# Attention of a two-layer kernel: the last five heads by halves of queries, nine scores in two slots, another end of the projection

## The reference, cut to what matters

```python
def _L0_attn_a_ref(x, Wk, Wq, Wv, Wu, bu):      # HEADS = 16, s = 8, t = 2048, e = 128
    scale = 1.0 / math.sqrt(s)
    keys = x @ jnp.triu(Wk).T                    # then reshaped to (b, t, h, s)
    queries = x @ jnp.tril(Wq).T
    values = x @ Wv.T
    dot = jnp.einsum('bqhs,bkhs->bhqk', queries, keys) * scale
    att = jax.nn.softmax(dot, axis=-1)
    out = jnp.einsum('bhqk,bkhs->bqhs', att, values).reshape(b, t, e)
    return out @ Wu.T + bu
x = x + _L0_attn_a_ref(_layernorm(x, axis=-1), ...)
x = x + _L0_ffn_ref(_layernorm(x, axis=-1), ...)
```

## Time and profile before

| | us |
|---|---|
| median of three runs | 1668.0 |
| the profiled execution's own time | 1668.66 |
| its span | 1666.9 |
| TensorE busy | 1519.7 (91%) |
| VectorE busy | 1383.8 (83%) |
| ScalarE busy | 920.8 (55%) |
| the tail, from the last maximum of the first pass (663.3) to the last instruction of the block (715.9) | 52.6 |

### The profile page before, as it was taken

How to read it: one execution, slowest core, us unless ns; L and a number is a source line. 1 busy time by engine, 2 the same in 40 slices (tenths; PEclk the granted TensorE clock), 3 DMA queues, 4 the chain that set the end, 5 groups by cost and what they waited for, 6 DMA issues and landing times. The chain is left out here.

```text
span 1666.9 us, 24179 instructions
## 1 busy us (share of the span) xinstructions
PE 1519.7 (91%) x8562; PEld 759.0 (46%) x8562; DVE 1383.8 (83%) x2459; ACT 920.8 (55%) x1751; POOL 296.9 (18%) x364
## 2 busy tenths in 40 slices
PE   6899999999999999979997888976999869989699
PEld 2111111111111111268883333322888758869587
DVE  6999999999999999476664999999766657787686
ACT  3088888888888888832224765754322232222232
POOL 3200000000000000000013788784000200020000
PEclk7599999999999999989998999999999979999799
DMA  3340000100000001000001222220000003200123
GB/s 95 102 159 24 24 30 27 31 27 25 24 24 24 24 24 49 9 1 1 1 1 41 73 64 72 67 67 26 1 1 1 1 1 103 81 23 1 52 78 103
DMA packets 41315, 65.92 MB, mean 40 GB/s; under 512 B 11444, under 2 KB 18661, under 8 KB 40490
## 3 DMA queue, kind: packets, MB, share of 16 engines
q1 hardware_dynamic: 41194, 64.37, 12.6%
HBM read 56.68 MB, written 6.75 MB: 38 GB/s over the span
## 5 line engine op out<-in xcount | busy, mean ns | idle before, releaser
L844 DVE TENSOR_REDUCE row_max<-ps 128x1 f32<-128x1024 f32 x512 | 601.2, 1220 | 33.4 <-PE ps L641 17.4
L758 ACT ACTIVATE probs<-ps 128x512 f32<-128x512 f32 x944 | 487.8, 603 | 119.7 <-PE ps L656 119.4
L641 PE MATMUL ps<-k_stack,q_stack 48*128 48x512 bf16 x1024 | 325.0, 402 | 20.4 <-DVE row_max L844 10.6
L656 PE MATMUL ps<-q_stack,k_stack 51*128 51x512 bf16 x944 | 322.1, 387 | 2.2 <-ACT probs L758 0.2
L585 PE MATMUL ps<-probs,v_head 128*16 128x512 f32 x2048 | 269.8, 599 | 1.3 <-issue 1.1
L641 PEld LDWEIGHTS ps<-k_stack,q_stack 48*128 48x128 bf16 x1024 | 58.5, 95 | 368.0 <-DVE row_max L844 342.0
L1373 PE MATMUL ps<-s_hc,ident 128*128 128x512 f32 x256 | 139.0, 628 | 47.9 <-DVE s_hc L1646 42.9
L1026 ACT ACTIVATE x_gate<-ps 128x512 f32<-128x512 f32 x128 | 76.5, 599 | 184.5 <-PE ps L122 184.4
L1298 POOL TENSOR_TENSOR s_dbx<-s_dx,s_b_rows 128x512 f32<-128x512 f32 x128 | 159.4, 1270 | 35.2 <-DVE s_h L1637 34.7
L1637 DVE TENSOR_TENSOR_SCAN s_h<-ps,s_state,s_dbx 128x512 f32<-128x512 f32 x128 | 157.3, 1274 | 4.6 <-POOL s_dbx L1298 2.8
L1063 DVE TENSOR_TENSOR x_hidden<-x_gate,ps 128x512 f32<-128x512 f32 x128 | 87.2, 686 | 53.4 <-PE ps L122 42.5
(11 more groups left out here) (345 smaller groups left out, 1935.1 us busy)
## 6 DMA issues: line engine op xcount, KB each, us to landing
s_b_rows<-s_b_dram SPq DMA_DIRECT2D x64, 256.0 KB, 3.1
y_spread<-y_probs_dram SPq DMA_DIRECT2D x128, 128.0 KB, 2.9
q_stack<-q_parts_dram SPq DMA_DIRECT2D x30, 96.0 KB
k_stack<-k_parts_dram SPq DMA_DIRECT2D x30, 96.0 KB
w_w<-w_dram SPq DMA_DIRECT2D x1, 2048.0 KB, 8.0
q_stack<-q_parts_dram SPq DMA_DIRECT2D x30, 64.0 KB
k_stack<-k_parts_dram SPq DMA_DIRECT2D x30, 64.0 KB
o_dram<-o_sb SPq DMA_DIRECT2D x60, 32.0 KB
```

Of the source, the lines that this page charges most:

```text
L641: last = nc.tensor.matmul(core.ps[:, 2 * b + r, :], qst[buf][0:KROWS, u * P:(u + 1) * P], kst[buf][0:KROWS, key:key + CH], start=True, sto ...
L656: nc.tensor.matmul(core.ps[:, S_BANK + n % S_RING, :], kst[buf][HALF:ROWS, kt * P:(kt + 1) * P], qst[buf][HALF:ROWS, c * CH:(c + 1) * CH], ...
L758: nc.scalar.activation(probs[:, us % RING, c * CH:(c + 1) * CH], core.ps[:, S_BANK + n % S_RING, :], ACT.Exp).then_inc(exp_done, 1)
L844: nc.vector.tensor_reduce(mx[:, u, b:b + 1], core.ps[:, 2 * b:2 * b + 2, :], mybir.AxisListType.XY, ALU.max).then_inc(max_done, 1)
```

## The change

The heads 11 to 15 go by halves of the queries: in the second pass, first all 16 key tiles for chunks 0 and 1, then all 16 for chunks 2 and 3, and the maxima of the 8 query tiles of a half are joined, turned, cut, stored and loaded by themselves. A score is then called an entry (1024 in all), and a list worked out ahead says how many are issued by the end of each slot: four more in every slot from 20, and a fifth in every even slot from 186 (HASTE), as far as the maxima are known by slot number (for a half of head h from slot 16h + 12 and 16h + 20). That makes 978 by slot 255, so that 46 are left for the tail. The fifth score stands behind the four pairs, ahead of the values.

The values of the halved heads go by groups of two entries: four matmuls of 256 columns for each (in place of four of 512 for a unit), eight entries behind the scores. So most slots have two groups; 14 even ones from 200 on have three, slot 196 has a whole unit and a group, slot 192 two whole units.

In the end, SyncE loads the 14 sums of weights alone as 112 rows of 256, VectorE takes one reciprocal of 112x256, SyncE stores it and loads it back spread over the eight rows of each head. The first half of head 15 is copied out (128x256) before its second half, and projected and added behind four of the tail's scores; `project_out` has two banks in turn and stands behind the scores with 9 and 5 left, behind the last score, and ahead of the last group of values. Only the second half of head 15 is left after the last exponent: one copy of 128x256, 8 small matmuls, four times a reciprocal and two tiles to add. The statistics and the tiles of the next norm's first chunk come ahead of that. The tail has five banks in place of six. The rolled numbering (bodies of 48 slots) is written out by entries; for heads 0 to 10 it gives the same order as before up to slot 185.

```diff
-    TAIL = UNITS - LAG_S
-    TAIL_BANKS, EARLY_OUT_BANK, LAST_TILES = (6, 4, 5, 0, 1, 2), 3, 3
-    OUT_UNITS = range(UNITS - NC_ - 1, UNITS - 1)
+    HALVED, HASTE = 11, 186
+    PAIR, QUARTER = 2, CH // 2
+    entries = [(head, kt, c) for head in range(HEADS)
+               for cs in (((0, 1), (2, 3)) if head >= HALVED else ((0, 1, 2, 3),))
+               for kt in range(NT) for c in cs]
+    def known_from(n):
+        head, half = n // OF_HEAD, n % OF_HEAD // OF_HALF
+        return head * NT + (LAG_S if head < HALVED else (half + 1) * (NT // 2) + LAG_S - NT)
+    issued = []
+    for gs in range(UNITS):
+        n = issued[-1] if issued else 0
+        if gs >= LAG_S:
+            most = n + NC_ + (gs >= HASTE and gs % 2 == 0)
+            while n < most and known_from(n) <= gs:
+                n += 1
+        issued.append(n)
+    TAIL = issued[-1]
+    TAIL_BANKS = tuple(S_BANK + (TAIL + i) % S_RING for i in range(S_RING)) + (0, 1)
+    LAST_HALF_BANK = 2
+    OUT_BANKS, END_BANKS = (3, 7), (0, 1, 4, 5)
...
             sp.wait_ge(o_stored, O_STORE * (HEADS - 2))
-            for which, dst in enumerate((attT, den)):
-                sp.dma_start(dst[0:MOST, :], od[which, 0:HEADS - 2]).then_inc(fin_loaded, 16)
-            store_max(HEADS - 1, (HEADS - 1) % NBUF)
-            store_o(HEADS - 2)
+            sp.dma_start(rden_rows[0:MOST, :],
+                         od[0:HEADS - 2, HD].rearrange("h (k n) -> h k n", n=QUARTER)).then_inc(den_loaded, 16)
+            sp.dma_start(attT[0:MOST, :], od[0:HEADS - 2, 0:HD]).then_inc(fin_loaded, 16)
+            store_max(LAST, 0)
+            store_max(LAST, 1)
+            sp.wait_ge(rden_ready, 1)
+            sp.dma_start(rdd.rearrange("h (k n) -> (h k) n", n=QUARTER), rden_rows[0:MOST, :]).then_inc(rden_stored, 16)
+            store_o(LAST - 1)
+            sp.wait_ge(rden_stored, 16)
+            sp.dma_start(den[0:MOST, :], rdd.unsqueeze(1).to_broadcast([HEADS - 2, HD, T])).then_inc(rden_loaded, 16)
...
+            def weigh_values(entry):
+                nonlocal weighed
+                while weighed < ENTRIES and weighed + group_size(weighed) <= entry:
+                    head, kt, c = entries[weighed]
+                    buf, half = head % NBUF, c // PAIR
+                    split = head >= HALVED
+                    bank = LAST_HALF_BANK if head == LAST and half else O_BANK
+                    if kt == 0 and c == 0:
+                        pe.wait_ge(v_staged, head + 1)
+                        if head:
+                            pe.wait_ge(evacuated, head)
...
+                    size = group_size(weighed)
+                    pe.wait_ge(exp_done, weighed + size)
+                    ring, at = weighed // NC_ % RING, weighed % NC_ * CH
+                    wide = size * CH // NC_
+                    out = half * wide if split and bank == O_BANK else 0
+                    for g in range(NC_):
+                        last = nc.tensor.matmul(core.ps[32 * g:32 * g + VROWS, bank, out:out + wide], v_head[buf][:, kt, :],
+                                                probs[:, ring, at + g * wide:at + (g + 1) * wide],
+                                                start=kt == 0, stop=kt == NT - 1)
+                    last.then_inc(pv_done, 1)
+                    weighed += size
...
+                first, end = issued[gs - 1] if gs else 0, issued[gs]
                 for c in range(NC_):
+                    find(c // 2, c % 2)
+                    if first + c < end:
+                        score(first + c)
+                for n in range(first + NC_, end):
+                    score(n)
+                weigh_values(end - 2 * NC_)
...
+            for n in range(TAIL, ENTRIES):
+                tail_score(n)
+                if n % 2:
+                    weigh_values(n + 1 - 2 * NC_)
+                left = ENTRIES - n
+                if left in (18, 17):
+                    project_first_half(18 - left)
+                if left in (14, 13):
+                    project_first_half(16 - left)
+                if left == 9:
+                    project_out(0)
+                if left == 5:
+                    project_out(1)
+            project_out(2)
+            weigh_values(ENTRIES - PAIR)
+            project_out(3)
+            weigh_values(ENTRIES)
+            pe.wait_ge(evacuated, HEADS + 1)
+            for g in range(NC_):
+                project_half(1, g, END_BANKS[g])
...
+            for n in range(ENTRIES):
+                head, kt, c = entries[n]
+                if n % OF_HEAD == 2 * NC_ and head:
+                    act.wait_ge(pv_done, group_of(head * OF_HEAD))
+                    if head > 1:
+                        act.wait_ge(o_stored, (head - 1) * O_STORE)
+                    nc.scalar.copy(o_sb[:], core.ps[:, O_BANK, :]).then_inc(evacuated, 1)
...
-            for c in range(NC_):
-                cols = slice(c * CH, (c + 1) * CH)
-                if c == 0:
-                    dve.wait_ge(fin_loaded, 32)
-                nc.vector.reciprocal(den[0:MOST, cols], den[0:MOST, cols]).then_inc(rden_ready, 1)
-                dve.wait_ge(rden_ready, c + 1)
+            dve.wait_ge(den_loaded, 16)
+            nc.vector.reciprocal(rden_rows[0:MOST, :], rden_rows[0:MOST, :]).then_inc(rden_ready, 1)
+            dve.wait_ge(fin_loaded, 16)
+            dve.wait_ge(rden_loaded, 16)
...
+            for g in range(NC_):
+                add_half(0, g, OUT_BANKS[g % len(OUT_BANKS)])
+            dve.wait_ge(half_added, 2 * NC_)
+            add_out(0)
+            dve.wait_ge(out_added, 1)
+            following.stat_rows(dve, 0)
+            add_out(1)
+            add_out(2)
             following.norm_rows(dve, 0)
+            add_out(3)
+            dve.wait_ge(out_added, NC_)
+            for g in range(NC_):
+                add_half(1, g, END_BANKS[g])
```

385 lines of the change are left out of this document (188 added, 197 removed).

## The result

**Slower, by about as much as forecast.** The median of the kernel after is 1679.34 us (1677.65 to 1682.16, 4 runs), that of the kernel before, measured beside it, 1667.39 (1666.19 to 1668.85, 4 runs): +12.0 us, ratio 1.0073, 95% interval 1.0055 to 1.0091. The prediction had +13.2, and 1681.

The account below looks back on a forecast made before the run. The prediction took a TensorE-ScalarE loop through three banks to bound each slot, with VectorE following. Main slots +28.9 and tail -15.7 gave +13.2 us on the median 1668.0, so 1681 us; own range 1673 to 1690, widened to 1666 to 1692.

Parts of the forecast that it names:

- The loop: Main slots: first score, its exponent, fourth score, values bind TensorE and ScalarE at 2.44 us a slot; VectorE follows.
- The fifth score: Even slots 186 to 254: waits for the second score's exponent, starts 0.48 later than the fourth did; +16.8 us.
- Values out of the tail: Main slots: 34 entries, 17 groups of 2 at 0.44 us each, move in from the tail; +7.5 us.
- Halved passes: Main slots: two more value passes per four entries, 0.013 us each, in some 60 slots; +1.6 us.
- rounds of maxima: Main slots: five more rounds of maxima at 0.1 us each; +0.5 us, ends 0 and 2.5.
- The copies: Main slots, heads 11 to 15: ScalarE's copies of bank 7 delay values or exponents; +2.8 us, ends 0 and 4.
- The tail: Last maximum to block end: 36.9 us against 52.6, with TensorE standing from T + 15 to T + 18.7; -15.7 us.
- the clock: Behind the block: gap shrinks to about 3 us, up to 3 us could be won, but 0 taken.
- VectorE's pace: Rival, main slots: VectorE paces them, so extra scores are hidden and the total is 1655 us; chance 0.14.
- a balance: Rival: even-slot waits partly taken up, tail gains 18 and clock 3; total within 0.2%, chance 0.06, slightly below 0.02.
- SyncE's order: Rival: SyncE's order holds maxima back until a slot stands; 1690 us and more, chance 0.03.
- Issue: Rival: issuing 16 value matmuls bounds halved slots, +0.5 us in 60 slots, 1711 us; chance 0.05.

Follow-up runs that it names:

- Experiment 2: Kernel before, each maximum taken over 512 of its 1024 columns, matmuls kept; 1657.90 us, one run.
- experiment 5: Kernel before, each slot's values weighed in two parts, half the columns behind the second find and score, half at the slot's end; 1629.66 us, ratio 0.9774.
- experiment 1: Kernel after without any fifth score (HASTE past the last slot), 80 entries left for the tail; 1667.73 us, ratio 1.0008.
- experiment 11: Kernel after, sums of heads 0 to 13 loaded spread out with `attT` and used undivided, no load back from DRAM; 1674.90 us, ratio 1.0044.
- experiment 6: Experiment 1's kernel with `project_out` sooner, tail values two groups at a time, head 14's output stored behind the spread load; 1663.20 us, ratio 0.9976.
- experiment 8: Kernel after, head 14's output stored between the last head's maxima so the spread load goes sooner; 1680.18 us, ratio 1.0079.

## Why the prediction was right, point by point

**What bounds a slot.** Right. The loop was read from the earlier trace rows against the waits, which named VectorE. Experiment 2 takes VectorE's load nearly in half and the slot stays; experiment 5 takes half of the values out of the loop and the slot falls to 2.27. The loop had forecast both; a VectorE that paced would have shortened every slot in the former and none in the latter.

**The fifth score.** The mechanism is shown (0.06 behind the second exponent). The size was 0.48 for each pair of slots, and measured is 2.93 + 2.40 - 2 x 2.444 = 0.44: the long slot is the 2.92 of the forecast, and the short one behind it gives back 0.04, since there VectorE waits and all four `find`s run without a stop. "The following slot of four gives nothing back" was the wrong sentence. Over the 35 pairs (two early ones have 0.37) it comes to some 15.2, where 16.8 was said. Slot 251 is 0.4 shorter, where 0.3 was said.

**Values out of the tail.** 0.44 a group was said, 0.43 measured: 7.3 for 7.5. **Halved passes** were +1.6 and **rounds of maxima** +0.5: experiment 1 has 0.5 for both in the five heads, and 0.9 with the second head. Two groups of values take 0.99, two passes took 0.98 (477.37 to 478.35). **The copies** and whatever else remains: 25.3 - 15.2 - 7.3 - 0.9 + 0.4 (slot 251) = 2.3, where +2.8 was said. The slots around the five copies are longer than their neighbours of the same kind by 0.9, 0.7, 0.1, 1.2 and 0.7, in all 3.7, but the 0.35 that each head of experiment 1 takes beyond its 16 slots (39.45 against 39.10) is gone from them. So the 3.6 too much in the first pass is 1.6 in the fifth scores, 1.2 in the passes and rounds, and the rest in small parts.

**The tail.** -15.7 was said, -11.4 came. Three steps of it: TensorE was to run into the wait at T + 15 and did so at T + 16.2 (1.2 of the 4.3), among others because the second half's maxima stopped it for 0.5. The load was said to take 5.5 like `attT` and took 7.6; the view behind the earlier trace rows has a second load of the same size, issued 0.37 us after that of `attT`, which took 7.7:

```profile
xnT<-o_dram SPq DMA_DIRECT2D x1, 896.0 KB, 7.7
```

As TensorE came later too, the standing of 3.7 was nevertheless the one forecast, and by luck. The step that failed, and the largest of the three, is the clock: "I take 0" looked only at the gap behind the block, and all work behind the new gap of 3.7 us was priced at rows of the 2.4 GHz level. The earlier trace rows had shown a low clock behind a gap; the gap that the change itself makes should have been given the same price. Measured from the third projection to the end, 21.25 against the forecast 18.2, and 18.1 in experiment 11, where the clock stays up: 3.1 of the 4.3.

**The rivals.** VectorE's pace and a balance: refuted. SyncE's order: no score of heads 11 to 15 outside the tail waits for loaded maxima. Issue: by rows 1711, refuted, since a third group adds 0.43 us for 8 matmuls, 0.054 us (54 ns) each, no more than a pass of the same columns took. The Trainium skill, TensorE: Matmul & The Clock Gate, section "Wait — 56ns, not 53.3ns?", gives about 62 ns of issue for each matmul with hardware decoding off; 54 ns a matmul is below that, so the bound is not at work here, and the trace does not tell which way of decoding was on.

**Both errors together.** 3.6 too much in the first pass and 4.3 too little in the tail leave 0.7 at the block's end. The total agrees for that reason, not because each term was right.

What stays open: why one slot of the second head takes 2.19 to 3.08 us, why the spread load took 7.6, and why the rest of the program takes between 946 and 951.5 us.

## What to carry to other kernels

Two engines at 96 to 98% busy need not be the limit: a ring of three banks between TensorE and ScalarE closed a loop that no busy share shows, and only the order of one slot's rows did. Before work is moved from an end to a main loop, ask what it costs there (0.49 for an exponent in the tail, 24.4 / 34 = 0.72 for one in the loop), and whether it can stand where the engine waits anyway; splitting a block of TensorE work and putting half of it ahead of a wait was worth 37.6 us, where the new end brought at most 4.8 (experiment 6 against 1). And a new standstill of TensorE is to be priced twice, once for itself and once for the clock behind it (3.7 and 3.1 here).

## What the runs showed of the hardware that I had not expected

- A load of 896 KB whose source is one row repeated over 8 partitions took 7.6 us from issue to use (7.55 in another kernel), with 128 KB of other loads beside it. Of two loads of that size with distinct rows, issued 0.37 apart in the kernel before, one landed after 5.5 us and one after 7.7. So the repeated row is not shown to be what made it slow.
- After 3.69 us of standing TensorE worked at the 1.2 GHz level for about 7 us; after 2.58 us of standing the clock fell as well (experiment 8), and after 1.61 us it was granted 0.80 and 0.77 in the two windows of 4 us from 676 on (experiment 1).
- Maxima of 1.22 us each can start 1.13 apart for a whole head, so a VectorE that is full shows 39.90 of 40 us, and one at 38.62 had 6% to give (39.34 to 36.84 a head).
- The same code behind the block took 946.1 to 951.5 us between profiled executions of these kernels, more than several of the effects studied.
- The page names the release of a wait by what came last: the first group of head 11's values waits in its record for GpSimd's copy of `v_head`, which had ended at 521.80, while the last thing it waited for was ScalarE's copy of bank 7 (from 521.48, 0.58 long, so to 522.06); the group starts at 522.16.
